# Attention of batches 1 to 3 with probabilities turned in blocks of 32 on VectorE and products over four row groups

## The chip, the cores and the metric

One core of a Trainium2 chip runs the whole kernel. Its engines are TensorE (matrix products into PSUM, 128 x 128), VectorE, ScalarE, GpSimd (POOL in the profile) and SyncE (SP), whose queue issues most transfers. They run on their own lists of instructions and meet only at semaphores. The metric is device time in microseconds (us), lower is better; the kernel before takes 131.04 us (median of 3 runs, 131.02 to 132.98).

## The reference

x has 4 batches of 512 tokens of 128 numbers, f32.

```python
# attention block
h = layernorm(x)                                  # over the last axis
q, k, v = h @ Wq + bq, h @ Wk + bk, h @ Wv + bv    # 128 -> 128
a = softmax(q @ k.T / sqrt(128)) @ v               # per batch, 512 x 512 scores
x = x + layernorm(a)
# mixture-of-experts block
h = layernorm(x)
spikes = sigmoid(h @ W_enc + b_enc)                # 128 -> 256
cont = spikes @ W_s2c + b_s2c                      # 256 -> 64
gate = two largest of softmax(cont @ Wr + br), scaled to sum 1, scattered over 8 experts
y = sum over e of gate[e] * (relu(cont @ W1[e] + b1[e]) @ W2[e] + b2[e])   # 64 -> 128 -> 64
d = sigmoid(y @ W_c2s + b_c2s) @ W_dec + b_dec     # 64 -> 256 -> 128
x = x + layernorm(layernorm(d) * ln_g + ln_b)
```

## The kernel before

**Tiling.** A batch is 4 groups (t) of 128 tokens. `x_in`, `x_mid` and the output keep tokens on the partitions; `xnT`, `yT`, `hT`, `spikes` and `cont` keep features on the partitions, turned by TensorE against an identity. All products are f32; an f32 product appears in the trace as two matmuls, each with its own weight load.

**Attention.** `project_y` makes yT, `project_v` v, `scores(b, t)` 128 x 512 scores in one of two PSUM banks. VectorE's `row_max` (L1200) takes the negative maximum, ScalarE's `exps` (L541) the exponentials with their sums, TensorE's `turn_probs` (L816) turns them as four squares of 128, ScalarE's `pT_out` (L546) copies them out of PSUM, and `attend` (L829) multiplies them with v: four products over 128 keys for each group. `attn_squares` (L552, ScalarE), `attn_var` (L1212, VectorE), a power of -1/2 on GpSimd (L431) and `mid_stats` (L1219, L1172 to L1177) add the normed result to x and take the statistics for the next norm.

**Experts.** `turn_h`, `encode` (L858), `to_cont`, `route` (L885), then `hidden_pair` (L918): the hidden layers of two experts, where two halves of the tokens lie on partitions 0 to 63 and 64 to 127. VectorE's `gate_hidden` (L1286) applies the bias, the relu and the gate, and `expert_out` (L942) sums eight experts in PSUM. `to_spikes`, `decode` (L971, L1002), `decode_scaled` and the two norms at the end follow. The router's gates go to HBM and come back spread over all partitions (`gate_all`, SP's queue). `router_top`, `router_index` and `router_gates` are VectorE's.

**Order.** Nothing is scheduled by a program: each engine's list of calls is written out by hand, and an engine never passes an instruction that waits. The batches are interleaved, so that attention of one batch stands between expert work of the batch two before it. An instruction waits for counts of semaphores (`wait_ge`), and so the order on one engine decides what the others get, and when. Small folds of biases (`b_cont`, `b_dec_sum`, `b2_plus`) are made on the way.

## Time and profile before

| | |
|---|---|
| median of 3 runs | 131.04 us |
| profiled execution | 130.91 us |
| its span | 129.0 us |
| TensorE busy | 118.7 us, 92% |
| VectorE busy | 94.4 us, 73% |
| ScalarE busy | 58.8 us, 46% |
| GpSimd busy | 33.8 us, 26% |
| granted TensorE clock, mean | 0.995 of full |

The span is the time from the first to the last recorded instruction of one profiled execution; the runs are timed around it. Busy time counts an engine's instructions, not its waits. Records of TensorE overlap, since one matmul begins while another ends: what a step costs is better read from the chain of waits, which goes back from the last instruction to what released it each time, or from the distance of two starts in the timeline. Groups by form give the mean length of one instruction. PE is TensorE, PEld its weight loads, DVE VectorE, ACT ScalarE.

### The profile page before, as it was taken

The page shows a single profiled execution, that of the slowest core. Times are in us where ns is not written, and L with a number is a line of the kernel's source. Part 1 is how long each engine was busy: PE and PEld are TensorE (multiplying, and loading weights), DVE is VectorE, ACT ScalarE, POOL GpSimd, SP SyncE. Part 2 cuts the span into 40 slices and gives each one's busy share as a digit, 9 for nine tenths or more (in the row PEclk, how much of TensorE's full clock was granted, in tenths as well). Part 3 has the DMA queues.
Part 4 walks back from the last instruction along what each step waited for, and adds up shares of the span by engine and source line. Part 5 has one row for each costly group of instructions (what it writes and reads, how often), then busy time and mean ns, then how long its engine had stood idle before and what let it go on. Part 6 is the DMA issues. An engine that isn't in the chain of part 4 may idle for free.

```text
span 129.0 us, 2501 instructions
## 1 busy us (share of the span) xinstructions
PE 118.7 (92%) x815; PEld 80.1 (62%) x815; DVE 94.4 (73%) x400; ACT 58.8 (46%) x173; POOL 33.8 (26%) x70
## 2 busy tenths in 40 slices
PE   6999999999999989999999999999998899998920
PEld 2556786878645767754575994657565455864910
DVE  0858537698989874788957168966889999389672
ACT  1647765556837575204666542053713003903620
POOL 4423503325231162220000132230081043330551
PEclk9999999999999999999999999999999999999998
DMA  3558800000000019700000198000019749720022
GB/s 113 132 121 227 234 18 3 0 0 3 0 5 0 0 50 324 290 8 0 0 0 0 41 293 329 3 0 0 8 48 319 299 138 323 276 86 0 4 79 81
DMA packets 9370, 12.42 MB, mean 96 GB/s; under 512 B 3169, under 2 KB 5998, under 8 KB 9358
## 3 DMA queue, kind: packets, MB, share of 16 engines
q1 hardware_dynamic: 8254, 12.08, 28.5%
q10 hardware_dynamic: 1104, 0.20, 0.8%
q8 instruction: 6, 0.10, 0.3%
q14 instruction: 6, 0.05, 0.1%
HBM read 11.16 MB, written 1.11 MB: 95 GB/s over the span
## 4 chain that ended last, share of the span: by engine, by line
PE 54%; DVE 23%; issue 8%; POOL 7%; ACT 3%; DMA 2%; POOLq 1%; DVEq 0%
PE ps_t L942 10%; POOL rstd L431 7%; PE ps_s L804 6%; PE ps_o L829 6%; PE ps_s L918 5%; PE ps_c L918 4%; DVE stats L1172 3%; PE ps_o L858 3%; PE ps_t L816 3%; DVE x_out L1366 2%; DMA x_in<-in_L_attn_x 2%; DVE xn L1184 2%; PE ps_o L918 2%; PE ps_a L769 2%; DVE neg_max L1200 2%
## 5 line engine op out<-in xcount | busy, mean ns | idle before, releaser
L431 POOL TENSOR_TENSOR rstd<-var_eps,minus_half 128x2 f32<-128x2 f32 (+1 forms) x33 | 25.4, 771 | 88.9 <-DVE var_eps L1177 47.3
L829 PEld LDWEIGHTS ps_o<-v,probsT 128*128 128x128 f32 x128 | 15.6, 191 | 4.6 <-ACT probsT L546 4.1
L829 PE MATMUL ps_o<-v,probsT 128*128 128x128 f32 x128 | 17.5, 279 | 0.4 <-ACT probsT L546 0.3
L942 PE MATMUL ps_t<-gated,w 128*64 128x256 f32 x128 | 17.0, 389 | 0.9 <-DVE gated L1286 0.8
L804 PE MATMUL ps_s<-xnT,yT 128*128 128x512 f32 x32 | 16.0, 596 | 0.1
L541 ACT ACTIVATE probs<-ps_s,neg_max 128x512 f32<-128x512 f32 x16 | 11.0, 687 | 11.1 <-DVE neg_max L1200 11.0
L1200 DVE TENSOR_REDUCE neg_max<-ps_s 128x1 f32<-128x512 f32 x16 | 10.9, 689 | 5.0 <-PE ps_s L804 4.9
L942 PEld LDWEIGHTS ps_t<-gated,w 128*64 128x64 f32 x128 | 8.0, 136 | 8.8 <-DVE gated L1286 4.2
L1286 DVE SCALAR_TENSOR_TENSOR gated<-ps_s,b_minus,gate_all 128x512 f32<-128x512 f32 x14 | 9.9, 744 | 1.9 <-PE ps_s L918 1.9
L546 ACT ACTIVATE probsT<-ps_t 128x512 f32<-128x512 f32 x16 | 9.5, 594 | 2.6 <-PE ps_t L816 2.4
L562 ACT ACTIVATE spikes<-ps_o,bias_half 128x512 f32<-128x512 f32 x6 | 4.1, 687 | 13.5 <-PE ps_o L858 13.4
L816 PE MATMUL ps_t<-ident,probs 128*128 128x128 f32 x64 | 9.8, 276 | 0.2 <-ACT probs L541 0.2
L816 PEld LDWEIGHTS ps_t<-ident,probs 128*128 128x128 f32 x64 | 7.3, 141 | 4.2 <-ACT probs L541 2.4
L1286 DVE SCALAR_TENSOR_TENSOR gated<-ps_c,b_minus,gate_all 128x512 f32<-128x512 f32 x12 | 8.4, 743 | 2.0 <-PE ps_c L918 2.0
L583 ACT ACTIVATE moeT<-ps_t 128x256 f32<-128x256 f32 x4 | 1.5, 384 | 14.5 <-PE ps_t L942 14.5
L918 PE MATMUL ps_s<-cont,w 64*128 64x256 f32 x56 | 7.9, 401 | 0.0
L804 PEld LDWEIGHTS ps_s<-xnT,yT 128*128 128x128 f32 x32 | 5.2, 191 | 2.7 <-issue 2.4
L1212 DVE SCALAR_TENSOR_TENSOR var_eps<-square_sum,eps_term 128x2 f32<-128x2 f32 x8 | 1.3, 165 | 7.1 <-ACT squares L552 6.9
L918 PE MATMUL ps_c<-cont,w 64*128 64x256 f32 x48 | 6.3, 380 | 0.0
L1219 DVE SCALAR_TENSOR_TENSOR x_mid<-ps_o,rstd,x_in 128x128 f32<-128x128 f32 x16 | 4.8, 343 | 2.0 <-POOL rstd L431 2.0
L918 PEld LDWEIGHTS ps_s<-cont,w 64*128 64x128 f32 x56 | 4.8, 186 | 2.1 <-issue 1.5
L1184 DVE TENSOR_SCALAR xn<-x_in,mean_var,rstd 128x128 f32<-128x128 f32 x16 | 5.2, 375 | 1.2 <-POOL rstd L431 0.9
(207 smaller groups left out, 218.6 us busy)
## 6 DMA issues: line engine op xcount, KB each, us to landing
gate_all<-gates SPq DMA_DIRECT2D x12, 512.0 KB, 6.0
gate_all<-gates SPq DMA_DIRECT2D x8, 256.0 KB, 3.6
x_in<-in_L_attn_x SPq DMA_DIRECT2D x3, 256.0 KB, 3.6
w<-in_L_ffn_W SPq DMA_DIRECT2D x3, 256.0 KB, 4.4
out<-x_out SPq DMA_DIRECT2D x3, 256.0 KB, 2.0
x_in<-in_L_attn_x SPq DMA_DIRECT2D x2, 128.0 KB, 2.5
out<-x_out SPq DMA_DIRECT2D x2, 128.0 KB, 1.7
w_enc<-in_L_ffn_W_enc SPq DMA_DIRECT2D x1, 128.0 KB, 2.7
```

The source lines that it names most:

```text
L431: nc.gpsimd.tensor_tensor(rstd[part], var_eps[part], minus_half[:, t0:t1], ALU.pow).then_inc(g_rstd[n], 1)
L541: nc.scalar.activation(probs[:, b % 2, t], ps_s[:, t % 2], ACT.Exp, bias=neg_max[:, b % 2, t:t + 1], accum_out=prob_sum[:, b % 2, t:t + 1] ...
L546: nc.scalar.activation(probsT[:, b % 2, t], ps_t[:, :].rearrange("p (k q) -> p k q", k=T), ACT.Identity).then_inc(a_pT, 1)
L804: nc.tensor.matmul(ps_s[:, t % 2], yT[:, b % 2, t * P:(t + 1) * P], xnT[:, b % 2], start=True, stop=True).then_inc(pe_s, 1)
L816: mm = nc.tensor.transpose(ps_t[:, k * P:(k + 1) * P], probs[:, b % 2, t, k * P:(k + 1) * P], ident[:, :])
L829: mm = nc.tensor.matmul(attn_out(t), probsT[:, b % 2, t, k], v[:, b % 2, k], start=(k == 0), stop=(k == T - 1))
L918: mm = nc.tensor.matmul(hidden_banks(b, e)[:, h], w1[half, e], cont[half, b % 2], start=True, stop=True)
L942: mm = nc.tensor.matmul(ps_t[h * M:(h + 1) * M, 0:SH], w2[:, e], gated[:, e, h * SH:(h + 1) * SH], start=False, stop=(e == E - 1))
L1184: nc.vector.tensor_scalar(result(t), source(t), mean_var[:, n, b % 2, t, 0:1], inv(n, b, t), ALU.subtract, ALU.mult).then_inc(done, 1)
L1200: nc.vector.tensor_reduce(neg_max[:, b % 2, t:t + 1], ps_s[:, t % 2], AX_X, ALU.max, negate=True).then_inc(v_max, 1)
L1219: nc.vector.scalar_tensor_tensor(x_mid[:, b, t], attn_out(t), inv(LN_ATT, b, t), x_in[:, b, t], ALU.mult, ALU.add).then_inc(v_mid, 1)
L1286: nc.vector.scalar_tensor_tensor(token_halves(gated[:, e]), hidden_banks(b, e), b1_minus[:, e:e + 1], token_halves(gate_all[:, b % 2, e]), ...
```

## The change

For batches 1 to 3 `turn_probs` and `pT_out` go. VectorE's `turn_blocks` transposes the 512 columns of one group's probabilities in squares of 32, which stay within their 32 partitions. With queries laid out in another order by `y_out`, this gives 16 pieces (`blocks[:, b % 2, j]`) in each of which every 32 partitions hold 32 keys against 128 queries. `attend(b)` is then 16 times four products of 32 rows, one for each quarter of the partitions; each quarter writes its own bank of `ps_o`, which has four banks now. Each quarter has to meet all keys, so v, with a column of ones that makes the sum of the probabilities, goes to HBM and comes back into all four quarters (`v_all`). ScalarE copies the result of a batch out of PSUM at once (`att_out`). Batch 0 stays as it was.

Along with it: for batches 2 and 3 the middle norm takes its squares on ScalarE (`mid_square`, `mid_var`, and `mid_add` in place of `mid_stats`); batch 0's last norm goes the way of batch 1's (ScalarE and GpSimd); bias folds stand together in `fold_biases`; output is written over `x_in`; PSUM banks are given out anew; and the lists of all engines are written in another order, in which scores and attention of a batch run ahead of the expert work of the one before.

```diff
+        v = sb("v", [P, 2, T, D + 1])
...
-        prob_sum = sb("prob_sum", [P, 2, T])
+        prob_sum = sb("prob_sum", [P, T])
...
-        probsT = sb("probsT", [P, 2, T, T, P])
+
+
+
+        blocks = sb("blocks", [P, 2, S // 32, T, 32])
+        v_all = sb("v_all", [P, 2, T, T, D + 1])
+
+        probsT = blocks[:, 0].rearrange("p (t a) b r -> p t a (b r)", t=T)
+        att = sb("att", [P, 2, T, D + 1])
```

```diff
+            sp.wait_ge(g_v_ones, 1)
+            for b in range(1, B):
+                sp.wait_ge(a_v, b + 1)
+                sp.dma_start(v_dram[b].ap(), v[:, b % 2].rearrange("p t d -> p (t d)")).then_inc(d_v_out[b], 16)
+                sp.wait_ge(d_v_out[b], 16)
+                if b == 3:
+                    sp.wait_ge(pe_o, 3)
+                for i in range(T):
+                    sp.dma_start(v_all[32 * i:32 * (i + 1), b % 2].rearrange("a j t d -> a j (t d)"),
+                                 v_dram[b].ap().rearrange("(j a) x -> a j x", j=T)).then_inc(d_v_all[b], 16)
 
             for b in range(B):
```

```diff
             def y_out(b):
                 for i, (bank, s0, s1) in enumerate(y_halves(b)):
                     act.wait_ge(pe_y, b + i + (b > 0) + 1)
-                    nc.scalar.activation(yT[:, b % 2, s0:s1], bank[:, s0:s1], ACT.Identity).then_inc(a_y, 1)
+                    if b == 0:
+                        nc.scalar.activation(yT[:, b % 2, s0:s1], bank[:, s0:s1], ACT.Identity).then_inc(a_y, 1)
+                    else:
+                        nc.scalar.activation(yT[:, b % 2].rearrange("d (t i r) -> d i t r", t=T, i=T),
+                                             bank[:, :].rearrange("d (i t r) -> d i t r", i=T, t=T),
+                                             ACT.Identity).then_inc(a_y, 1)
...
             def exps(b, t):
                 act.wait_ge(v_max, T * b + t + 1)
-                nc.scalar.activation(probs[:, b % 2, t], ps_s[:, t % 2], ACT.Exp, bias=neg_max[:, b % 2, t:t + 1],
-                                     accum_out=prob_sum[:, b % 2, t:t + 1]).then_inc(a_exp, 1)
-
-            def pT_out(b, t):
-                act.wait_ge(pe_pT, T * b + t + 1)
-                nc.scalar.activation(probsT[:, b % 2, t], ps_t[:, :].rearrange("p (k q) -> p k q", k=T),
+                nc.scalar.activation(probs[:, b % 2, t], ps_s[:, t % 2], ACT.Exp,
+                                     bias=neg_max[:, b % 2, t:t + 1],
+                                     accum_out=prob_sum[:, t:t + 1] if b == 0 else None).then_inc(a_exp, 1)
...
+            def att_out(b):
+                act.wait_ge(pe_o, b + 2)
+                if b == 3:
+                    act.wait_ge(v_mid, 2 * T)
+                nc.scalar.activation(att[:, b % 2], ps_o[:, :, 0:D + 1], ACT.Identity).then_inc(a_att, 1)
...
+            def mid_square(b, h):
+                act.wait_ge(v_mid, T * b + TH * (h + 1))
+                for t in range(TH * h, TH * (h + 1)):
+                    nc.scalar.activation(squares[:, b % 2, t], x_mid[:, b, t], ACT.Square, scale=-1.0,
+                                         bias=mean_var[:, LN_X, b % 2, t, 0:1],
+                                         accum_out=mid_square_sum[:, b % 2, t:t + 1]).then_inc(a_mid_square, 1)
```

```diff
+            def attend(b):
+                pe.wait_ge(v_blocks, T * b)
+                pe.wait_ge(d_v_all[b], 16 * T)
+                if b == 1:
+                    pe.wait_ge(v_mid, T)
+                    pe.wait_ge(a_square, T)
+                elif b == 2:
+                    pe.wait_ge(a_att, 1)
+                    pe.wait_ge(v_b2, 1)
+                    pe.wait_ge(v_bdec, 1)
+                    pe.wait_ge(v_bcont, 1)
+                    pe.wait_ge(v_logit, 1)
+                else:
+                    pe.wait_ge(v_gated, E)
+                for j in range(S // 32):
+                    for i in range(T):
+                        rows = slice(32 * i, 32 * (i + 1))
+                        mm = nc.tensor.matmul(ps_o[:, i, 0:D + 1], blocks[rows, b % 2, j].rearrange("p t r -> p (t r)"),
+                                              v_all[rows, b % 2, j % T, j // T],
+                                              start=(j == 0), stop=(j == S // 32 - 1))
+                mm.then_inc(pe_o, 1)
...
+            def fold_biases():
+                pe.wait_ge(a_att, 1)
+                pe.wait_ge(g_s2c, 1)
+                for h in range(2):
+                    for c in range(HC):
+                        mm = nc.tensor.matmul(ps_o[h * M:(h + 1) * M, 0, 0:1], w_s2c[:, c], ones[:, 0:1],
+                                              start=(c == 0), stop=(c == HC - 1))
+                pe.wait_ge(v_b1, 2)
+                pe.wait_ge(d_w2, 32)
+                for e in range(E):
+                    mm = nc.tensor.matmul(ps_o[0:E, 1, 0:M], b1_diag[:, e], w2[:, e], start=(e == 0), stop=(e == E - 1))
+                mm.then_inc(pe_b2, 1)
+                pe.wait_ge(v_wdec, 8)
```

```diff
+            def turn_blocks(b, t):
+                dve.wait_ge(a_exp, T * b + t + 1)
+                if b >= 2:
+                    dve.wait_ge(pe_o, b)
+                nc.vector.transpose(blocks[:, b % 2, :, t], probs[:, b % 2, t]).then_inc(v_blocks, 1)
```

ScalarE's list and part of TensorE's (its new calls):

```diff
+            att_out(1)
+            act.wait_ge(v_bias2, 2)
+            hT_out(0)
+            attn_squares(1, 0)
+            exps(2, 2)
+            attn_squares(1, 1)
+            spike(0, 0)
+            spike(0, 1)
+            exps(2, 3)
+            xnT_out(3)
+            cont_out(0)
+            y_out(3)
+            second_exp(0)
+            values_out(3)
+            att_out(2)
+            exps(3, 0)
+            attn_squares(2, 0)
```

```diff
+            project_y(2)
+            scores(2, 0)
+            project_v(2)
+            scores(2, 1)
+            attend(1)
             turn_h(0)
-            turn_probs(1, 3)
-            attend(1, 2)
+            fold_biases()
+            scores(2, 2)
             encode(0, 0)
             encode(0, 1)
-            attend(1, 3)
-            turn_x(2)
+            scores(2, 3)
             to_cont(0)
-            project_y(2)
+            turn_x(3)
             route(0)
-            scores(2, 0)
-            scores(2, 1)
-            project_v(2)
```

VectorE, from the middle of batch 1 to the first gated experts:

```diff
+            x_stats(3)
+            turn_blocks(2, 0)
+            turn_blocks(2, 1)
             attn_var(1, 0)
+            row_max(2, 2)
+            mid_stats(1, 0)
+            attn_var(1, 1)
+            x_norm(3)
+            row_max(2, 3)
+            mid_norm(1, 0)
+            mid_stats(1, 1)
...
+            turn_blocks(2, 2)
+            turn_blocks(2, 3)
+            mid_norm(1, 1)
+            router_top(0)
+            router_index(0)
+            router_gates(0)
+            row_max(3, 0)
+            attn_var(2, 0)
+            row_max(3, 1)
+            mid_add(2, 0)
+            attn_var(2, 1)
+            turn_blocks(3, 0)
+            mid_add(2, 1)
+            turn_blocks(3, 1)
+            mid_var(2, 0)
+            router_top(1)
+            row_max(3, 2)
+            gate_hidden(0, 0)
```

Places where the order moves, as the built programs have it. The first is TensorE around the projections of batch 3 (`xnT,w_a` is `project_y`, `wv,xnT` is `project_v`, `xnT,yT` a score, `ident,hn` a turn of h, `hT,w_enc` an encode, `w_r,cont` the route). Before:

```order
L777 MATMUL ps_a<-xnT,w_a 128x512
L829 MATMUL ps_o<-v,probsT 128x128 x4
L787 MATMUL ps_a<-wv,xnT 128x128 x4
L918 MATMUL ps_s<-cont,w 128x256 x4
L918 MATMUL ps_c<-cont,w 128x256 x4
L936 MATMUL ps_t<-gateT,b_plus 64x256 x2
L942 MATMUL ps_t<-gated,w 64x256 x8
L918 MATMUL ps_s<-cont,w 128x256 x4
```

and with the change:

```order
L948 MATMUL ps_o<-w_r,cont 128x8 x4
L827 MATMUL ps_a<-xnT,w_a 128x512
L837 MATMUL ps_a<-wv,xnT 128x128 x4
L894 MATMUL ps_o<-v_all,blocks 128x129 x64
L852 MATMUL ps_s<-xnT,yT 128x512 x2
L909 MATMUL ps_a<-ident,hn 128x128 x4
L923 MATMUL ps_o<-hT,w_enc 128x512 x2
L992 MATMUL ps_o<-cont,w 128x256 x4
L936 MATMUL ps_a<-spikes,w_s2c 64x256 x4
```

The projections stand behind the route of batch 0, batch 2's attention is one block of 64 products behind them, and the encode of batch 1 comes right after, ahead of all hidden experts; before, the turn of h of batch 1 had been made among the attention steps, and hidden experts came first.

The second is ScalarE at the same place (`hT` is the copy that an encode waits for, `squares` those of the attention norm, `att` the copy of the attention's result). Before, in the like place for batch 3's attention:

```order
L587 ACTIVATE spikes<-ps_c,bias_half 128x512 x2
L546 ACTIVATE probsT<-ps_t 128x512
L573 ACTIVATE e<-top_diff 128x4
L541 ACTIVATE probs,prob_sum<-ps_s,neg_max 128x512
L557 ACTIVATE hT<-ps_a 128x512
L546 ACTIVATE probsT<-ps_t 128x512
L578 DMA gates<-gate_blocks 4x32x32
```

and with the change, behind batch 2's attention:

```order
L634 ACTIVATE e<-top_diff 128x4
L578 ACTIVATE v<-ps_a 128x4x128
L597 ACTIVATE att<-ps_o 128x516
L584 ACTIVATE probs<-ps_s,neg_max 128x512
L605 ACTIVATE squares,square_sum<-att 128x128 x2
L639 DMA gates<-gate_blocks 4x32x32
L584 ACTIVATE probs<-ps_s,neg_max 128x512
L605 ACTIVATE squares,square_sum<-att 128x128 x2
L618 ACTIVATE hT<-ps_a 128x512
L623 ACTIVATE spikes<-ps_o,bias_half 128x512 x2
```

The copy of hT of batch 1 now has two exponentials and two pairs of squares ahead of it, all of which belong to batch 2 or 3.

The third is VectorE, where `b_cont` is made, for which ScalarE's first copy of `cont` waits. Before:

```order
L1200 TENSOR_REDUCE neg_max<-ps_s 128x1
L1219 SCALAR_TENSOR_TENSOR x_mid<-ps_o,rstd,x_in 128x128 x2
L1172 BN_STATS stats<-x_mid 128x6 x2
L1175 BN_AGGR mean_var<-stats 128x2 x2
L1177 TENSOR_SCALAR var_eps<-mean_var 128x2
L1200 TENSOR_REDUCE neg_max<-ps_s 128x1
L1408 TENSOR_SCALAR w_dec<-w_dec_raw,dec_mean 128x128 x2
L1411 TENSOR_TENSOR b_cont<-ps_c,bias_cols 128x1
L1414 TENSOR_SCALAR b_minus<-bias_cols 128x8
L1415 COPY b_diag<-bias_cols 128x8
```

and with the change:

```order
L1243 TENSOR_REDUCE neg_max<-ps_s 128x1
L1284 TENSOR_SCALAR hn<-x_mid,mean_var,rstd 128x128 x2
L1266 SCALAR_TENSOR_TENSOR x_mid<-att,rstd,x_in 128x128 x2
L1215 BN_STATS stats<-x_mid 128x6 x2
L1218 BN_AGGR mean_var<-stats 128x2 x2
L1220 TENSOR_SCALAR var_eps<-mean_var 128x2
L1505 TENSOR_TENSOR b_cont<-ps_o,bias_cols 128x1
L1507 SCALAR_TENSOR_TENSOR b_dec_sum<-b_dec_all,dec_mean,ps_o 128x128
L1511 TENSOR_TENSOR b_plus<-ps_o,b_rows 8x64
L1292 STREAM_TRANSPOSE blocks<-probs 128x16x32 x2
```

It stood behind the second maximum of batch 1 and stands now behind both middle blocks of batch 1.

## Rows read from the trace of the kernel before

**Rows 1.** The page, part 1: busy us, share of span, instructions.
```profile
PE 118.7 (92%) x815; PEld 80.1 (62%) x815; DVE 94.4 (73%) x400; ACT 58.8 (46%) x173; POOL 33.8 (26%) x70
```

**Rows 2.** The chain of waits, TensorE: start us, us, engine, tile, line, matmuls.
```profile
47.92 0.90 PE ps_o L829 x8
48.82 0.44 PE ps_t L816 x4
...
51.10 0.89 PE ps_a L787 x8
...
53.06 0.86 PE ps_c L918 x8
...
58.47 1.91 PE ps_o L858 x4
60.38 1.72 PE ps_s L804 x4
62.10 1.88 PE ps_t L942 x16
...
75.63 0.95 PE ps_o L829 x8
```

**Rows 3.** Timeline of weight loads (start us, us, ...); line 1033 (ns min/median/max).
```profile
17.71 0.32 PEld L1033 LDWEIGHTS ps_c<-ones,w_s2c 128*64 128x64 f32 x8
...
L1033 PEld LDWEIGHTS ps_c<-ones,w_s2c x8: 133/137/138, 17.7 to 17.9; 128*64 128x64 f32 x8
```

**Rows 4.** Timeline of VectorE, 31 to 40 us: start us, us, instruction, count.
```profile
31.43 1.11 DVE L1184 TENSOR_SCALAR xn<-x_in,mean_var,rstd 128x128 f32<-128x128 f32 x4 [0.45 <-POOL rstd L431]
...
36.71 0.61 DVE L1219 SCALAR_TENSOR_TENSOR x_mid<-ps_o,rstd,x_in 128x128 f32<-128x128 f32 x2 [0.33 <-POOL rstd L431]
37.35 0.49 DVE L1172 BATCH_NORM_STATS2 stats<-x_mid 128x6 f32<-128x128 f32 x2
...
38.09 0.17 DVE L1177 TENSOR_SCALAR var_eps<-mean_var 128x2 f32<-128x2 f32 x1
38.17 0.19 DVE L1232 TENSOR_TENSOR logits<-ps_c,br_all 128x32 f32<-128x32 f32 x1
...
38.88 1.28 DVE L1200 TENSOR_REDUCE neg_max<-ps_s 128x1 f32<-128x512 f32 x2
```

**Rows 5.** Groups by form: busy us, mean ns, idle before.
```profile
L546 ACT ACTIVATE probsT<-ps_t 128x512 f32<-128x512 f32 x16 | 9.5, 594 | 2.6 <-PE ps_t L816 2.4
...
L1299 DVE TENSOR_TENSOR z<-ps_a,g_all 128x512 f32<-128x512 f32 x2 | 1.4, 687 | 0.0
...
L1259 DVE TENSOR_TENSOR pick<-expert_no,top_no 128x32 f32<-128x32 f32 x8 | 1.2, 187 | 0.2
...
L1277 DVE STREAM_TRANSPOSE gate_blocks<-gate 128x32 f32<-128x32 f32 x4 | 0.8, 212 | 0.1
```

**Rows 6.** Timeline, 19 to 25 us: a score, its maximum, exponential, squares.
```profile
19.04 1.02 PE L804 MATMUL ps_s<-xnT,yT 128*128 128x512 f32 x2
...
20.10 0.69 DVE L1200 TENSOR_REDUCE neg_max<-ps_s 128x1 f32<-128x512 f32 x1 [0.83 <-PE ps_s L804]
...
23.02 0.69 ACT L541 ACTIVATE probs<-ps_s,neg_max 128x512 f32<-128x512 f32 x1 [0.92 <-DVE neg_max L1200]
...
24.17 0.28 ACT L552 ACTIVATE squares<-ps_o 128x128 f32<-128x128 f32 x1
...
24.58 0.22 ACT L552 ACTIVATION_READ_ACCUMULATOR squares<-ps_o 128x1 f32 x1
```

**Rows 7.** The chain of waits, VectorE: first and last step of batch 2's router.
```profile
89.06 0.20 DVE logits L1232
...
92.17 0.21 DVE gate_blocks L1277
```

**Rows 8.** Timeline: the last gated experts; page part 6: issues, KB, us to landing.
```profile
114.75 1.41 DVE L1286 SCALAR_TENSOR_TENSOR gated<-ps_o,b_minus,gate_all 128x512 f32<-128x512 f32 x2 [0.59 <-PE ps_o L918]
...
gate_all<-gates SPq DMA_DIRECT2D x8, 256.0 KB, 3.6
```

More of the change, by code:

```diff
@@ L259, in attention_moe_block @@
         d_ln = sem("d_ln")
+        d_v_out = [sem(f"d_v_out{b}") for b in range(B)]
+        d_v_all = [sem(f"d_v_all{b}") for b in range(B)]
         d_gateT = [sem(f"d_gateT{i}") for i in range(2)]
@@ L464, in _ @@
                 inverse_std(LN_MID, 1, h)
-            inverse_std(LN_X, 3, 0)
+            for h in range(2):
+                inverse_std(LN_ATT, 2, h)
+            for h in range(2):
+                inverse_std(LN_MID, 2, h)
             pool.wait_ge(v_wdec, 8)
@@ new lines, in _ @@
+            exps(3, 1)
+            attn_squares(2, 1)
+            hT_out(1)
+            spike(1, 0)
+            spike(1, 1)
+            mid_square(2, 0)
+            cont_out(1)
+            exps(3, 2)
+            mid_square(2, 1)
+            second_exp(1)
+            exps(3, 3)
+            hT_out(2)
+            spike(2, 0)
+            spike(2, 1)
+            gate_out(1)
+            moe_out(0)
+            att_out(3)
+            attn_squares(3, 0)
+            cont_out(2)
+            spike2(0, 0)
@@ L1039, in _ @@
-            attend(0, 2)
+            turn_probs(3)
+            attend_first(2)
             scores(1, 1)
-            turn_probs(1, 0)
-            attend(0, 3)
+            attend_first(3)
             scores(1, 2)
-            turn_probs(1, 1)
-            attend(1, 0)
-            pe.wait_ge(v_wdec, 8)
-            pe.wait_ge(v_bias, 1)
-            for c in range(HC):
-                mm = nc.tensor.matmul(ps_c[:, 0, 0:D], ones[:, :], w_dec[:, c], start=(c == 0), stop=(c == HC - 1))
-            mm.then_inc(pe_bdec, 1)
@@ new lines, in _ @@
+            project_y(3)
+            project_v(3)
+            attend(2)
+            scores(3, 0)
+            scores(3, 1)
+            turn_h(1)
+            encode(1, 0)
+            encode(1, 1)
+            hidden_pair(0, 0)
+            to_cont(1)
+            scores(3, 2)
+            route(1)
+            expert_biases(0)
+            hidden_pair(0, 1)
+            scores(3, 3)
+            for e in range(4):
+                expert_out(0, e)
+            turn_h(2)
+            hidden_pair(0, 2)
@@ new lines, in _ @@
+            hidden_pair(0, 3)
+            encode(2, 0)
+            encode(2, 1)
+            for e in range(4, E):
+                expert_out(0, e)
+            attend(3)
+            to_cont(2)
+            to_spikes(0)
+            route(2)
+            hidden_pair(1, 0)
+            expert_biases(1)
+            hidden_pair(1, 1)
+            decode(0)
+            for e in range(4):
+                expert_out(1, e)
+            hidden_pair(1, 2)
+            turn_h(3)
+            hidden_pair(1, 3)
@@ L1122, in _ @@
             expert_out(1, 4)
             expert_out(1, 5)
-            to_cont(2)
+            encode(3, 0)
+            encode(3, 1)
             expert_out(1, 6)
             expert_out(1, 7)
-            route(2)
+            to_cont(3)
+            to_spikes(1)
             hidden_pair(2, 0)
-            to_spikes(1)
-            encode(3, 0)
-            encode(3, 1)
-            decode(1, 0)
-            decode(1, 1)
-            to_cont(3)
-            decode(1, 2)
-            decode(1, 3)
@@ L1148, in _ @@
-            expert_out(2, 7)
+            to_spikes(2)
             hidden_pair(3, 1)
-            to_spikes(2)
             expert_biases(3)
-            decode_part(2, 0)
+            for e in range(4):
+                expert_out(3, e)
+            decode(2)
             hidden_pair(3, 2)
-            expert_out(3, 0)
-            expert_out(3, 1)
             hidden_pair(3, 3)
-            for e in range(2, E):
+            for e in range(4, E):
                 expert_out(3, e)
@@ L1160, in _ @@
             for h in range(2):
-                decode_part(3, h)
+                decode(3, h)
             for h in range(2):
@@ L1482, in _ @@
-            attn_var(3, 1)
-            for e in range(1, 4):
-                gate_hidden(1, e)
-            mid_stats(3, 1)
-            mid_norm(3, 0)
+            attn_var(3, 0)
+            mid_add(3, 0)
+            attn_var(3, 1)
+            router_top(2)
+            mid_add(3, 1)
+            gate_hidden(1, 0)
+            gate_hidden(1, 1)
+            router_index(2)
+            mid_var(3, 0)
+            gate_hidden(1, 2)
+            mid_var(3, 1)
+            router_gates(2)
+            mid_norm(3, 0)
@@ L1513, in _ @@
             z_means(1, 0)
+            scaled_weights()
             for e in range(E):
```

592 lines of the change are left out of this document (243 added, 349 removed).

## The prediction

> **What bounds the kernel now.** I read four views, in this order. The page's busy line [rows 1]: TensorE works 92% of the span, VectorE 73%, ScalarE 46%. The chain of waits [rows 2] is mostly TensorE in its middle, and gives what TensorE's steps cost when they follow each other: attention of one group of tokens 0.90 us, its turn 0.44, one pair of hidden experts 0.86, two scores 1.72, two encodes of the same columns behind a change of mode 1.91, four expert outputs 1.88. The timeline [rows 3, 4, 6, 7] gives the pace inside a step, which is a little less than the mean length of one instruction, because ends overlap. The groups by form [rows 5] give lengths that no step isolates. The reader is to see that TensorE is the bound, and that it can be only because VectorE and ScalarE are always one step ahead of it. The profiled execution took 130.91 us with a span of 129.0, so 1.9 lie around the span; the median of the runs is 131.04.
>
> **The change, part by part.**
>
> *Turns off TensorE.* Twelve turns of probabilities go (batches 1 to 3): 12 x 0.44 = 5.3 us of TensorE [rows 2]. ScalarE loses their 12 copies, 12 x 0.59 = 7.1 us [rows 5]. It gains three copies of the attention's result (0.6 each by the same row), squares for the middle norms of batches 2 and 3 (0.63 for two with their sums: 24.17 to 24.80 [rows 6]) and batch 0's last normalisation. At 46% its total decides nothing; its order does, below.
>
> *The new attention.* 64 products of 32 rows for each batch. An f32 product runs as two matmuls, here of 129 columns; before, eight matmuls of 128 took 0.90, so 0.112 each. Two row groups do run side by side: eight matmuls of 256 columns took 0.86, where four of 512, the same columns in sequence, took 1.72 [rows 2]. Four abreast, a batch is 128 x 0.112 / 4 = 3.6 us; two abreast 7.2; one at a time 14.3. I take 3.6. Four abreast need a new matmul every 0.028 us, and eight tiny ones were issued in 0.32 less the last one's own 0.14, so 0.026 apart [rows 3]. That is the nearest row, and it is close. So attention costs TensorE what it cost (4 x 0.90).
>
> The Trainium skill ("TensorE: Matmul & The Clock Gate", Part 3, the table of measured speedups) has four row tiles at 3.07 times, not 4. By that a batch takes 4.7 us and the sum grows by about 3. No row here has four groups.
>
> *Turns on VectorE.* Twelve block transposes of 512 columns. Those of the trace have 32: 212 ns, where arithmetic on 32 columns takes 187 and on 512 takes 687 [rows 5]. That is 1.04 ns a column, so 212 + 480 x 1.04 = 0.71 us. If instead all above a base of 147 were columns, 2.0 ns each, it would take 1.2; below, nothing of 512 columns paces under 0.6 [rows 4]. I take 0.71, in sequence 0.66, because the longer base fits what 32 columns show beside their neighbour. VectorE gets 12 x 0.66 = 7.9 us, loses the statistics of eight groups (0.74 a pair by the rows from 37.35 to 38.09, so 3.0) and batch 0's last centring and sum, some 2.5: net +2.4 on 94.4. Again the place decides, since six of the turns fall before 40 us.
>
> *v through HBM.* Out 264 KB once, back four times 264 KB; a 256 KB fetch took 3.6 us to land [rows 8], and as the four share the engines I put both ways at 8 to 10 us together. In the walk below each v is ready 13 us or more before its use: nothing. Without that cover it would be up to 8 us. The gate fetches stand behind these on SP's queue; the last v fetch is through by about 58, when batch 0's gates leave: nothing.
>
> *Memory shared anew* (x_in as output, one ps_o of four banks): nothing, their readers are long done; if one were not, a wait of one step, 0.9.
>
> **The walk.** The engines hand work to each other in another rhythm now, so I follow the new order with these prices. Up to 17.5 us nothing differs.
>
> (a) *To the end of batch 2's attention.* VectorE from 17.5: statistics of x 1.3, five maxima 3.2, four turns 2.6, x norm 1.1, two middle blocks of 1.46 (36.71 to 38.17), small ones 1.1, and 2.8 of waits for scores: the fourth turn of batch 1 ends at 32.5 [rows 4]. Its attention: 32.5 to 36.3, copied by 37.2, then the bias folds 1.6 and a score, and the next maximum starts at 40.0. From there VectorE has 0.65 + 1.46 + 0.3 + 1.1 + 0.6 + 0.55 + 1.46 = 6.1 ahead of b_cont, which is now formed last: 46.1. cont of batch 0 waits for b_cont on ScalarE, route for cont, and batch 3's projections stand behind route on TensorE: 0.5 + 0.5 + 0.9 + 0.8 for the copy + 0.9, so 49.7. Batch 2's attention: 49.8 to 53.4. Before, that attention and batch 3's v were both through at 52.0 [rows 2]. With 8 turns, 3.5 us, saved, it is 1.4 later, and the turn of h of batch 1 (0.44), done before, is still to come.
>
> (b) *Behind it.* encode(1) needs hT(1), which ScalarE copies only after this: score 0.9 and 0.2 to land, maximum 0.65, exponential 0.65, squares 0.63, a small VectorE step 0.2, the second maximum 0.65, exponential 0.65, squares 0.63, the copy 0.6, together 5.8 [rows 2, 4 to 6]. TensorE has 2.2 of work in between, stands for 3.6, and goes on at 59.2.
>
> (c) *To the end of batch 3's attention.* encode 1.7, hidden 0.9, cont 0.9, a score 0.9 and route with its copy: 64.1. VectorE: top of the router 0.7 and 0.2 to land, 65.0; then to the last gated expert of batch 0 eight gated 5.4 (0.68 each [rows 8]), two turns and two maxima 2.6, middle norms 1.1, index 0.6, the router's gates 1.5 (a whole router took 89.06 to 92.38, some of it a wait [rows 7]; I take 2.8), 0.15: 76.4. Its product ends at 77.6 behind an encode, attention at 81.4. Before, this was 76.6 [rows 2]. What is left for TensorE then is 1.1 more now (to_spikes and decode of batch 0 against an encode).
>
> (d) *To the last gated expert.* TensorE has 12 hidden pairs 10.3, 24 expert outputs 11.3, three decodes 6.0, an encode 1.7, five steps of 0.86, routes, biases and a turn 2.5: 36.1, with some 2.2 for changes of mode (0.19 between 1.91 and 1.72, less for short steps) 38.3, to 119.7. To this come hand-offs where VectorE is late: gated(1,3) behind the gates of router 2, 2.5; gated(2,4) to (2,7) behind router 3 and a scaling, 1.6; scaled_weights, now ahead of all of batch 3's, 2.5: 6.6 in all, so the last gated expert ends at 125.8. Before it ended at 116.2 [rows 8], 39.6 after the attention. At that stretch's losses it would now be 81.4 + 39.6 + 1.1 = 122.1.
>
> (e) *The end.* Before, 116.2 to 129.0 = 12.8; less the scaling of batch 2, which now stands ahead: 12.2.
>
> Sum: 125.8 + 12.2 = 138.0 of span, or 134.3 by the milder form of (d); with 2.0 around it up to the median, 140.0 and 136.3. I forecast **138**, between them: 5% slower.
>
> **The rivals.** *TensorE alone is still the bound* and the waits of (a) to (d) are covered; this one ends on the other side. The 5.3 us of turns fall out, six changes of mode (0.19) are added: 131.0 - 5.3 + 1.1 = 126.8. The 92% speak for it. It decides from the point where the wait before encode(1) is under 0.5 us, and a chain of ten steps stands there: 14%.
>
> *The late part wins the early loss back*: batch 2's attention ends at 53.4, but (b) overlaps and (d) runs without late hand-offs. Then attention of batch 3 ends at 77 to 79, and 38.3 + 12.2 + 2 behind it give 130 to 132: 13%.
>
> *Row groups go only two abreast*, or the sequencer can't feed four: 3.6 more for each batch, 10.7, part of it in TensorE's idle time of (a): 145 to 149. The pace of 0.026 speaks against it: 8%.
>
> *Dear transposes*: 12 x 0.5 = 6, two thirds of it on the chain: 142. The trace has none beyond 32 columns: 9%.
>
> My forecast keeps 56%. That the change isn't done can be left out: the order of instructions has the twelve transposes and three times 64 products in their places.
>
> **How the numbers follow.** A difference of 2% is about what can be told from none here. Slower by over 2%: 0.56 + 0.08 + 0.09 = 0.73; within 2%: 0.13; faster: 0.14. The range goes from 130, where the win-back ends, to 143, which takes in dear transposes; outside lie TensorE as the only bound and most of two abreast, some 20% together.
>
> **What would show it.** Right: 3.6 to 4.0 us for a batch's attention in the chain; transposes of 0.7; TensorE idle for 3 us or more before encode(1), waiting for hT, and some 2 before batch 0's route; the last gated expert past 121. Wrong: batch 2's attention over before 51, encode(1) within a microsecond of the turn of h, or waits for gated experts no longer than before.

## The result, and the profile after

The changed kernel takes 152.97 us (median of 5 runs, 151.99 to 157.02) against 131.04 (5 runs, 130.95 to 132.98): a ratio of 1.165 [1.160, 1.171]. It is 16.5% slower; 138 was forecast, 5% slower, and the range ended at 143. The direction was right, the time was not. Some executions of a kernel run longer at a lower granted clock (157.02 us here, at 0.896 where the other four had 0.922 to 0.927); the ratios leave them out.

The changed kernel was profiled again beside the experiments, in an execution of 152.87 us (span 151.1), and all its rows here are from that one. The page, part 1 and the row of the granted clock (tenths, 40 slices of 3.8 us):

```profile
PE 124.3 (82%) x1054; PEld 78.5 (52%) x1054; DVE 96.2 (64%) x387; ACT 57.8 (38%) x172; POOL 34.8 (23%) x72
...
PEclk9999999599999689959977999996999999999985
```

TensorE's share fell from 92% [rows 1] to 82%, yet it is busy 5.6 us longer, though 5.3 us of turns are gone, and its idle time grew from 10.3 us (129.0 - 118.7) to 26.8. The clock row says why it is busy for longer: it dips five times before the end. The chain of waits, in order of time (start us, us, engine, tile, line, count):

```profile
33.76 3.83 PE ps_o L894 x128
...
47.16 0.16 DVE b_cont L1505
47.41 0.48 ACT cont L630
47.93 0.61 PE ps_o L948 x8
...
50.29 2.07 PE ps_a L837 x8
52.36 4.43 PE ps_o L894 x128
56.80 1.07 PE ps_s L852 x2
...
62.05 0.50 ACT hT L618
62.59 2.49 PE ps_o L923 x4
...
83.92 1.88 PE ps_t L1013 x16
85.80 3.78 PE ps_o L894 x128
```

L894 is the new attention: 3.8 us a batch, as forecast. Batch 3's v (L837, x8) takes 2.07 us, the same work as 0.89 in [rows 2]: it ran at the lower clock. So did part of the attention behind it and of the encode at 62.59. The windows table shows the clock beside TensorE's busy time (us, then busy and count of PE, PEld, DVE, ACT, POOL, then clock):

```profile
26.00:30.00 4.00, 4.00 (x8) 1.54 (x8) 2.35 (x8) 1.39 (x3) 0.06 (x1) 0.57 0.59 117
30.00:44.00 14.00, 13.01 (x183) 8.85 (x184) 10.42 (x42) 6.52 (x18) 2.96 (x4) 1.00 0.39 96
...
77.00:81.00 4.00, 3.74 (x18) 2.49 (x20) 2.07 (x11) 0.60 (x1) 0.00 (x0) 0.57 0.00 0
81.00:86.00 5.00, 5.00 (x38) 2.57 (x38) 4.03 (x10) 1.53 (x3) 0.00 (x0) 1.00 0.02 3
```

A mean of 0.57 over 4 us is 3.4 us at 1.2 GHz and 0.6 at 2.4. With 48 to 58, 61 to 72 and 100 to 110 us (0.83; 0.87 and 0.83; 0.83) the lower level holds for 17 us. What comes ahead of each stretch is in the list of waits, the last of which end at 25.9, 47.9, 62.6, 77.3 and 100.0 us (engine and tile, whom it waited for: us, times, longest):

```profile
PE ps_t L1013 <- DVE gated L1352: 7.5, 6, 1.9
PE ps_o L923 <- ACT hT L618: 3.4, 1, 3.4
PE ps_o L948 <- ACT cont L630: 2.3, 1, 2.3
PE ps_a L819 <- DVE xn L1227: 2.2, 1, 2.2
```

The end, on the chain:

```profile
129.96 1.80 PE ps_a L1051 x16
...
131.96 0.97 ACT squares L661 x7
132.93 1.53 ACT z L668 x4
134.53 1.26 POOL x_in L470
135.79 0.25 POOL b_z_hi L518
...
138.31 1.03 POOL rstd L459
```

z of batch 1 (L668) could have been normalised from 125.5 us on, when POOL had its factors ready and ScalarE was about to stand idle until 131.8, but it stands in ScalarE's list behind the squares of batch 2's decode; POOL adds it, then forms the bf16 parts of b_z (2.4 us), and only then batch 2's rstd.

### The profile page after: what moved, and what is told of

Same layout as the page of the kernel before. It is cut to its first block, busy times and chain, and to the rows that moved or that the text cites. A ratio compares the mean times of both kernels' runs of the same rounds, so it can differ in the third digit from the quotient of the medians.

```text
span 155.2 us, 2982 instructions
## 1 busy us (share of the span) xinstructions
PE 128.5 (83%) x1054; PEld 81.1 (52%) x1054; DVE 96.2 (62%) x387; ACT 57.9 (37%) x172; POOL 34.8 (22%) x72
## 4 chain that ended last, share of the span: by engine, by line
PE 58%; DVE 21%; ACT 7%; POOL 5%; issue 4%; DMA 2%; POOLq 1%; ACTq 0%; DVEq 0%
PE ps_o L894 9%; PE ps_s L852 7%; PE ps_o L992 6%; PE ps_t L1013 6%; DVE gated L1352 4%; DVE neg_max L1243 3%; PE ps_a L827 3%; POOL rstd L459 3%; PE ps_a L837 2%; PE ps_s L923 2%; PE ps_o L923 2%; PE ps_a L1051 2%; DVE stats L1215 2%; PE ps_a L936 2%; DMA w_qkv<-in_L_attn_Wk 2%
## 5 line engine op out<-in xcount | busy, mean ns | idle before, releaser
L1352 DVE SCALAR_TENSOR_TENSOR gated<-ps_o,b_minus,gate_all 128x512 f32<-128x512 f32 x24 | 16.8, 743 | 7.8 <-PE ps_o L992 7.8
L992 PE MATMUL ps_o<-cont,w 64*128 64x256 f32 x96 | 15.8, 464 | 0.0
L894 PEld LDWEIGHTS ps_o<-v_all,blocks 32*128 32x128 f32 x384 | 13.0, 215 | 1.4 <-DVE blocks L1292 0.8
L894 PE MATMUL ps_o<-v_all,blocks 32*128 32x129 f32 x384 | 13.6, 302 | 0.0
L992 PEld LDWEIGHTS ps_o<-cont,w 64*128 64x128 f32 x96 | 10.4, 225 | 4.7 <-issue 2.6
L923 PE MATMUL ps_o<-hT,w_enc 128*128 128x512 f32 x8 | 5.7, 846 | 3.4 <-ACT hT L618 3.4
L1292 DVE STREAM_TRANSPOSE blocks<-probs 128x512 f32<-128x512 f32 x12 | 8.2, 696 | 0.0
L1051 PEld LDWEIGHTS ps_a<-w_dec,spikes 128*128 128x128 f32 x48 | 5.9, 192 | 0.1
L1051 PE MATMUL ps_a<-w_dec,spikes 128*128 128x128 f32 x48 | 5.8, 275 | 0.0
L1352 DVE SCALAR_TENSOR_TENSOR gated<-ps_s,b_minus,gate_all 128x512 f32<-128x512 f32 x8 | 5.7, 741 | 0.0
```

The costliest lines, as they stand in the source:

```text
L894: mm = nc.tensor.matmul(ps_o[:, i, 0:D + 1], blocks[rows, b % 2, j].rearrange("p t r -> p (t r)"), v_all[rows, b % 2, j % T, j // T], star ...
L923: nc.tensor.matmul(enc_bank(b, c), w_enc[:, c * P:(c + 1) * P], hT[:, b % 2], start=True, stop=True).then_inc(pe_enc, 1)
L992: mm = nc.tensor.matmul(hidden_banks(b, e)[:, h], w1[half, e], cont[half, b % 2], start=True, stop=True)
L1051: mm = nc.tensor.matmul(decoded(b, t), spikes2[:, b % 2, c, t * P:(t + 1) * P], w_dec[:, c], start=False, stop=(c == HC - 1 and t == t1 - 1))
L1292: nc.vector.transpose(blocks[:, b % 2, :, t], probs[:, b % 2, t]).then_inc(v_blocks, 1)
L1352: nc.vector.scalar_tensor_tensor(token_halves(gated[:, e]), hidden_banks(b, e), b1_minus[:, e:e + 1], token_halves(gate_all[:, b % 2, e]), ...
```

## The experiments

Times are medians; beside these kernels the kernel before took 131.2 to 131.3 us, and gains are counted from the 152.87 of the changed kernel's second profile. Theories: **clock** (TensorE's gaps are followed by stretches at 1.2 GHz, for which my sum had no term), **order** (hand-offs late by the place of an instruction in a list), **end** (POOL's and ScalarE's last lists), and the rival, that **the new operations** themselves (products, transposes) cost.

**Gaps filled.** 58 products of zeros, as the warm-up's, at seven places (12 + 10 of them among the expert outputs of batches 0 and 1; the 48 of the text below leaves ten out). One of the places:

```diff
+ def fill(bank, count):
+     for _ in range(count):
+         nc.tensor.matmul(bank, zeros[:, 0:P], zeros[:, :], start=True, stop=True)
  pe.wait_ge(a_att, 2)
+ fill(ps_o[:, 0], 12)
  encode(1, 0)
```

> The changed kernel with 48 bf16 products of zeros (128x512, as the warm-up's) in TensorE's gaps: 8 before turn_x(2), 4 before scores(2,0), 8 before route(0), 4 before project_v(3), 12 before encode(1,0), 12 between the first four expert_out of batch 0 and 10 before expert_out(1,2) and (1,3). Each writes a bank that stands free and that the next product there overwrites; nothing is left out. Changed kernel: 152.5 us. Clock theory (TensorE is granted 1.2 GHz after each of five gaps, and some 27 us of the trace pass at that level, in which TensorE is behind by about half): the PEclk row shows 9 all through from the start to the last 5 us and the time falls by 8 to 13 us, to 140 to 144. Order theory (the lists make TensorE late, the clock only shows it): the gaps are as long as before, the clock may be up, but what follows a gap waits on the other engines anyway: 150 to 153. If the fillers only cost (48 by 0.2 us, those that don't fit in their gap): 153 to 158.

147.20 us, 1.122 [1.114, 1.130]: 5.7 less than the changed kernel, from work that computes nothing. The row of the clock, and the attention of batches 2 and 3 in its chain:

```profile
PEclk9999999999999999999999999999999999995599
...
49.96 3.78 PE ps_o L900 x128
...
79.58 3.78 PE ps_o L900 x128
```

Attention of batch 3 ends at 83.4 instead of 89.6. Nothing but the fillers and the clock differs up to there, and the fillers compute nothing, so the clock is shown to cost about 6 us. The first 1.5 of them are less certain (attention 1 starts at 32.29 for 33.76): other executions, below, kept the clock behind that first gap without a filler. The gain misses the 8 to 13 expected, which counted 27 us at the lower level from the 157.02 us execution; the one of 152.87 has 17, worth 8.5 at most. By the last gated expert the gain is 7.2 us (130.0 for 137.1), and 0.6 is lost behind it, where this kernel has a dip of its own.

**Two hand-offs earlier.**

```diff
  row_max(2, 2)                  # VectorE
+ dve.wait_ge(pe_bdec, 1)
+ (b_cont)
  mid_stats(1, 0)
  attend(2)                      # TensorE
+ turn_h(1)
  scores(3, 0)
  att_out(2)                     # ScalarE
+ hT_out(1)
  exps(3, 0)
```

> The changed kernel with two moves: b_cont with its wait for pe_bdec on VectorE right after row_max(2,2) (it stood 5 us later, behind mid_stats(1,1)), and turn_h(1) on TensorE ahead of scores(3,0) with ACT's hT_out(1) right behind att_out(2). Order theory: the gap of 2.4 us before route(0) shrinks to 1 or less and that of 3.6 us before encode(1,0) goes: 5 to 6 us less by the gaps alone, 146.5 to 148. Clock theory adds that the two falls that follow them (47.7 to 58 us and 64.8 to 71.6 us) go too, worth another 5 to 8 us: 139 to 143. If it is the attention or the transposes themselves that cost, the time stays at 150 to 153.

145.21 us, 1.108 [1.100, 1.116]: 7.7 less. The wait for hT(1) is gone from the list, that for cont is 1.4 instead of 2.3, and the clock's row has lost the dips at 48 and 61 us:

```profile
PEclk9999999999999999999789999959999999997797
...
49.24 3.78 PE ps_o L894 x128
```

More than the gaps (0.9 + 3.4) came back, as the clock theory said, but the time lies between the ranges of the two theories (139 to 143 and 146.5 to 148): a shallower one follows at 68 to 75 us, and one at 93. And 1.3 us are not the moves' own: the gap before turn_x(2), the same in both kernels, is followed by a dip at 26 us in the changed kernel and by none here, so attention 1 starts at 32.44 for 33.76. That leaves 6.4 for the moves.

**The end's order.**

```diff
  spike2(2, c)                   # ScalarE
+ z_norm(1)
  dec_square(2, 0)
- z_norm(1)
- scaled_weights()               # VectorE, ahead of gate_hidden(3, *)
+ scaled_weights()               # ahead of attn_var(3, 0)
  (b_z chain on POOL: ahead of inverse_std(LN_DEC, 0, 0))
```

> The changed kernel with the end's order alone changed: VectorE's scaled_weights ahead of attn_var(3,0) (it stood ahead of batch 3's gated products), POOL's b_z chain ahead of the LN_DEC of batch 0, and ACT's z_norm(1) ahead of dec_square(2,0). Tail theory (z_norm(1) behind dec_square(2,0) holds POOL's z_add(1), and behind it stand 2.5 us of b_z chain and the rstd of batch 2): 2.1 us from the gated products of batch 3 and about 4 us behind decode(2): 145.5 to 148. Theory that the end is set by TensorE's late products alone: at most the 2.1 us of VectorE, 150 to 151.5. If the moved work only delays batch 3's attention norms: 152 to 155.

Four runs took 147.49, 148.52, 152.50 and 153.73 us. The first, which was profiled, and the second are 4 to 5 less than the changed kernel; two are too few for an interval, and the rows have to answer. POOL's timeline:

```profile
126.90 1.27 POOL L470 TENSOR_TENSOR x_in<-z,x_mid 128x512 f32<-128x512 f32 x1 [1.76 <-ACT z L668]
132.57 1.02 POOL L459 TENSOR_TENSOR rstd<-var_eps,minus_half 128x4 f32<-128x4 f32 x1 [4.39 <-DVE var_eps L1372]
```

The sum of batch 1 comes 7.6 us earlier and batch 2's rstd waits for its variance, not for POOL. From the last gated expert to the end it is 11.9 us (133.8 to 145.7), where the changed kernel has 14.0 (137.1 to 151.1). The last gated experts:

```profile
132.40 1.40 DVE L1352 SCALAR_TENSOR_TENSOR gated<-ps_s,b_minus,gate_all 128x512 f32<-128x512 f32 x2
```

against, in the changed kernel:

```profile
135.73 1.40 DVE L1352 SCALAR_TENSOR_TENSOR gated<-ps_s,b_minus,gate_all 128x512 f32<-128x512 f32 x2
```

Of the 5.4 us between the spans 2.1 is the end, and 2.6 lies between the end of attention 3 and the last gated expert (88.8 to 133.8 for 89.6 to 137.1), where `scaled_weights` was moved away. The rest, 0.7, was there before any move, in an execution that kept its clock at 26 us. So the moves themselves are worth 4.7.

**Both sets of moves.**

> The moves of the two kernels before this one together. If gaps, clock and tail are separate causes, the gains add: 152.5 less 9 to 14 (order with clock) less 5 to 7 (tail) is 132 to 138, the forecast's own 138 at the upper end. If the order moves are worth their gaps alone, 140 to 143. If neither matters, 150 or more.

140.64 us, 1.074 [1.066, 1.081]: 12.2 less, nearly the sum of the two (7.7 and about 5): by the rows 6.4 and 4.7 from the moves, and 1.3 from the dip at 26 us, which this execution did not have either. The gains add, but each was smaller than expected: not 132 to 138, but the low end of the range for moves worth their gaps alone. A dip at 70 us remains, and one at 90 to 97.

**Both, and its gaps filled** (34 products of zeros).

> Both moves of the kernel before (140.6 us) with 34 products of zeros in the gaps that it still has: 8 before turn_x(2), 5 before route(0), 12 between the first expert_out of batch 0, 9 before expert_out(1,3). That kernel's trace shows 1.2 GHz at about 67 to 72 us and 94 to 99 us, some 6 us in all. Clock theory: 9 all through in the PEclk row and 2 to 3 us less, 137.5 to 139. Order theory (the waits of the lists decide what is left): 140 to 141. Fillers that don't fit: over 141.

137.83 us, 1.047 [1.036, 1.058], and 9 in all slices of the clock but the last (the page is of an execution of 139.31 us). 2.8 us less, as the clock theory said.

**Fewer transposes.** Both moves, without turn_blocks of batches 2 and 3:

```diff
- turn_blocks(2, *), turn_blocks(3, *)
- pe.wait_ge(v_blocks, T * b)
+ pe.wait_ge(v_blocks, T)
+ pe.wait_ge(a_exp, T * (b + 1))
```

> Both moves (140.6 us) without VectorE's eight block transposes of batches 2 and 3: their attention reads the blocks of batches 0 and 1, so the probabilities of those two batches are left out of the result. It takes 8 by 0.70 us = 5.6 us off VectorE. Theory that the transposes on VectorE are what delays the hand-offs (norms, gated products, router) around 42 to 75 us: 3 to 5 us less, 136 to 138. Theory that VectorE has room beside TensorE and the order of the lists decides: 139.5 to 141.

1.086 [1.071, 1.101]; the two runs that the ratio rests on took 140.39 and 141.34 us, against 140.64: with 5.6 us less work on VectorE nothing is won. One thing hides in this: the profiled execution has the dip at 27 us, which that with both moves has not, and attention 2 starts 1.5 us later for it (50.75 for 49.29). So the transposes may be worth up to some 1.5 us, but not the 3 to 5 of their theory; each took 0.70 us:

```profile
L1292 DVE STREAM_TRANSPOSE blocks<-probs 128x512 f32<-128x512 f32 x12 | 8.2, 697 | 0.0
```

(that row is of the changed kernel: busy us, mean ns, idle before.)

**One hole in the kernel before.**

```diff
  act.wait_ge(v_max, T * b + t + 1)          # exps(2, 2)
+ act.dma_start(hole[:, :], bq...).then_inc(d_hole, 16)
  (attend(2, 0), TensorE)
+ pe.wait_ge(d_hole, 16)
```

> The kernel before the change (131.0 us) with one hole: TensorE waits ahead of attend(2,0), where its trace has no gap over 0.5 us for 20 us, for a small DMA that ACT issues once row_max(2,2) is done; nothing is left out. The gap should be 2.5 to 4 us. Clock theory: the granted clock, which never falls in that kernel until its last microseconds, falls to 1.2 GHz behind the hole for some 3 us, and the time rises by the gap and 1.5 to 2 us more, 135 to 137, unless waits further down take part of it back. Theory that the fall has another cause than a gap (what kind of products run, four row groups): the clock stays up, and the time rises by the gap or less, 132 to 135.

**The same hole, filled** with 12 products of zeros.

> The kernel before with the same hole and 12 bf16 products of zeros (some 2.6 us at full clock) in it. Clock theory: the clock stays up, and the time is 1.5 to 2 us below that of the empty hole. If the clock doesn't matter, both are alike, within 0.5 us.

135.36 us, 1.031 [1.021, 1.042], and 134.09, 1.023 [1.010, 1.036]. The step behind the hole, then 46 to 50 us, first empty:

```profile
45.61 1.38 PE L835 MATMUL ps_o<-v,probsT 128*128 128x128 f32 x8 [3.69 <-DMA hole<-in_L_attn_bq]
...
46.00:50.00 4.00, 4.00 (x18) 3.18 (x17) 0.00 (x0) 1.19 (x2) 0.91 (x2) 0.57 0.01 2
```

and filled:

```profile
45.81 1.16 PE L837 MATMUL ps_o<-v,probsT 128*128 128x128 f32 x8 [0.70 <-DMA hole<-in_L_attn_bq]
...
46.00:50.00 4.00, 4.00 (x32) 3.46 (x31) 1.26 (x4) 1.62 (x3) 1.20 (x3) 1.00 0.03 6
```

In a kernel with none of the change's operations a gap of 3.7 us alone brings the clock down: TensorE is busy all 4 us in both, and does 18 matmuls in one, 32 in the other. The medians differ by 1.3 us and the spans by 1.4, a little below the 1.5 to 2 expected. The two intervals overlap, but the mean clock was 0.977 to 0.981 in the four runs with the empty hole and 0.989 to 0.999 in the four with the filled one. The hole costs 4.1 us empty and 2.8 filled.

**The products one after another.** Both moves, with attend's loops exchanged, so that neighbours share their 32 rows:

```diff
- for j in range(S // 32):
-     for i in range(T):
+ for i in range(T):
+     for j in range(S // 32):
```

> The kernel with both moves (140.6 us) with the two loops of attend exchanged: all 16 products of a row group, then those of the next, so that no two that follow one another stand on different rows. The same products, loads and bytes, nothing left out. In the kernel with both moves one batch takes 3.85 us. If the overlap of products on different rows is what makes 64 products of 32 rows no dearer than 16 of 128, one batch now takes 12 to 15 us, and the time is about 3 by 9 to 11 us longer, 160 to 172, less what falls into gaps. If it made no difference, 3.9 us a batch and 140 to 141.

205.06 us (one run): further than expected, since here the clock falls with no gap ahead. The chain's step for batch 1, and its windows:

```profile
32.36 20.45 PE ps_o L894 x128
...
36.00:38.00 2.00, 2.00 (x23) 2.00 (x20) 0.11 (x1) 0.00 (x0) 0.00 (x0) 1.00 1.04 239
38.00:42.00 4.00, 4.00 (x25) 4.00 (x24) 0.00 (x0) 0.00 (x0) 0.00 (x0) 0.51 0.74 149
42.00:46.00 4.00, 4.00 (x23) 4.00 (x24) 0.00 (x0) 0.00 (x0) 0.00 (x0) 0.50 0.00 0
```

The overlap is real: 3.8 us side by side, 20.5 in sequence. At the upper clock the sequence would take 128 x 0.112 = 14.3 us [rows 2], and the first 5.6 us have its pace, so four abreast is about 3.8 times as fast.

**Batch 0's router ahead of attention 1**, as before the change.

> The kernel with both moves (140.6 us) with batch 0's encoder and router ahead of attention 1, as they were before the change: turn_h(0), scores(2,2), encode(0,*), fold_biases, to_cont(0), scores(2,3), turn_x(3), route(0), attend(1) on TensorE, VectorE's and ACT's lists in the same order, gate_out(0) ahead of att_out(1). In the kernel with both moves route(0) runs at 45.8 us, the first gate_all lands after 64 us, and TensorE waits for gated products 0.7, 2.6 and 0.5 us between 66 and 70 us. Late-gates theory: route(0) at about 41, the gate_all there before hidden_pair(0,0), these gaps and the fall of the clock behind them gone: 4 to 6 us less, 135 to 137. Theory that batch 0's place doesn't matter, as TensorE has other work meanwhile: 139.5 to 141. If attention 1, now 5 to 8 us later, holds batch 1's encoder: 142 to 145.

142.28 us, 1.083 [1.073, 1.093]: not faster than 140.64, so the late-gates theory fell as it stood; the value is in the range of the third, and TensorE now waits 1.7 us for hn before batch 1's turn of h. route(0) ran 5 us earlier and its gates left 10 us earlier, but SyncE's queue and VectorE's list did not use them (the chain's row of gate_out, the timelines of SyncE and VectorE):

```profile
45.25 1.07 ACTq L639
...
52.82 1.73 SPq L418 DMA_DIRECT2D v_all<-v  x4
54.65 0.28 SPq L429 DMA_DIRECT2D gateT<-gates  x1
54.97 2.23 SPq L431 DMA_DIRECT2D gate_all<-gates  x5
...
65.38 0.74 DVE L1357 SCALAR_TENSOR_TENSOR gated<-ps_o,b_minus,gate_all 128x512 f32<-128x512 f32 x1
```

The fetch stands behind v_all(3). That does not wait for attention 2, as the next text has it: in the kernel it needs `pe_o` at 3, the end of attention 1, and in the trace SyncE's queue stood 13.2 us for v(3), which ScalarE had ready at 50.0, and 2.4 for its way to HBM. The first gated expert stands behind router_top(1).

**Batch 0's experts first**: the fetch ahead of v_all(3), its hidden pairs, gated products and outputs ahead of encode(1,*) and router_top(1).

```diff
+ fetch_gates(0)                 # SyncE, ahead of sp.wait_ge(pe_o, 3)
  scores(3, 0)                   # TensorE
+ hidden_pair(0, 0); hidden_pair(0, 1); expert_biases(0)
  turn_h(1)
  ...
+ (expert_out(0, *), hidden_pair(0, 2), hidden_pair(0, 3))
  encode(1, 0)
```

> The kernel of the early router (142.3 us) with batch 0's experts ahead of batch 1's encoder and router, as before the change: SyncE fetches batch 0's gates ahead of v_all(3) (whose issue waits for attention 2), TensorE runs hidden_pair(0,*) and expert_out(0,*) from behind scores(3,0) on and encode(1,*) behind them, VectorE the eight gated(0,*) from behind row_max(3,0) on, router_top(1) behind them. In the early-router kernel route(0) ran 5 us earlier and its gates left at 45 us, but the first gated product stood behind router_top(1) on VectorE and the fetch behind v_all(3) on SyncE, and it came at 65.4 us all the same. Theory that the place of batch 0's experts is what the rest of the loss is: the last gated product of batch 0 comes at 62 to 66 us instead of 76 to 78, TensorE's gaps at 66 to 71 us go, and the time is 133 to 137. Theory that the work only changes places (batch 1's encoder now comes late in its stead, with gaps of its own at 60 to 75 us): 140 to 145.

138.00 us, 1.054 [1.045, 1.062], the fastest without fillers: 2.6 less than both moves alone and 4.3 less than the early router. Batch 0's last gated expert comes at 68.0 (76.4 with both moves, 60.9 before the change), and the clock stays up, in this execution: three took 137.96 to 138.04 us at a mean clock of 0.992 to 0.994, the fourth 139.36 at 0.980. The page's row, attention 3, and the last gated experts of all:

```profile
PEclk9999999999999999999999999999999999999997
...
76.74 3.79 PE ps_o L899 x128
...
122.51 1.40 DVE L1364 SCALAR_TENSOR_TENSOR gated<-ps_s,b_minus,gate_all 128x512 f32<-128x512 f32 x2
```

That is later than its theory's 62 to 66 and 133 to 137, and better than its rival's 140. The fetch itself went only 1.8 us earlier (52.86 for 54.65), since it still stands behind v(3)'s way to HBM. Against the kernel before, attention 3 ends 4.0 us later (80.5 for 76.6), from there to the last gated expert it is 3.8 more (43.4 for 39.6), and the end is 0.5 shorter.

**The changed kernel again**, whose rows stand above.

> The changed kernel itself once more, beside the others on one chip, for its profile. All theories: 151 to 154 us, with the granted clock at 1.2 GHz behind each gap of over 2 us on TensorE (about 26, 48, 65, 80 and 104 us), a clock of about 0.92 over the span.

152.87 us, clock 0.926, the gaps where they were expected.

No version beats the kernel before.

## Why the prediction was wrong, by its own steps

**Turns, attention, transposes** were right. Attention 3.8 us a batch for 3.6; the trace bears out four groups abreast. Its 3.8 times is not the 3.07 of the Trainium skill's table ("TensorE: Matmul & The Clock Gate", Part 3), which is for 512 columns where this kernel has 129; the 4.7 us estimated from it no batch took at the upper clock. Transposes 0.70 for 0.71. Fewer of them won at most 1.5 us. v through HBM never held TensorE.

**(a) and (b), the hand-offs**, were right in kind. b_cont at 47.2 for 46.1; TensorE stood 3.4 us before encode(1) for 3.6, and from the score at 56.80 to the encode at 62.59 it was 5.8, the 5.8 forecast. What failed is what stood around them: attention 2 ended at 56.8, not 53.4.

**The step that failed is one that the sum does not have: TensorE's clock in the stretches behind its waits.** I priced each step of (a) to (d) by rows of a kernel whose clock never fell in its middle, while the same walk took gaps of 2 and 3.6 us into TensorE's work. With the gaps filled, attention 2 is at 49.96 to 53.74, where 49.8 to 53.4 was forecast, and attention 3 ends at 83.4 for 81.4. The fall costs 5.7 us of the 14.9 by which the forecast missed (152.87 less 138). Which of the gaps brings it was partly chance: the first, before turn_x(2), not in every execution.

**(c)** came at 89.6 for 81.4; 6.2 of the 8.2 is that clock, 2.0 is left. With the gaps filled, encode(2) ends at 77.7, and four expert outputs stand whole behind it in TensorE's list (1.9 us), where the walk had the last of them end at 77.6.

**(d)** was 44.4 us long by the sum; 47.5 in the changed kernel (89.6 to 137.1), 46.6 with the gaps filled. (Its own terms, 38.3 and 6.6, add up to 44.9: the walk says 125.8 where 126.3 comes out.) scaled_weights was priced rightly: with it moved, the stretch is 45.1 with both moves, where it was 47.6 with the hand-offs alone. The stretch was under-sized by 2.2, by which of the other hand-offs no run separates, and its milder form, by which I had taken 2 us off the sum of 140.0, had nothing for it.

**(e)** was 12.2 and measured 14.0, with the gaps filled 14.6 (a dip at 130 to 137 us lies in it, so some 0.6 of this is clock too); with the lists mended 11.9. I carried the old end over, less one scaling, and did not follow POOL, which now forms b_z and batch 2's rstd behind z_add(1).

Together, from 138: clock 5.7, (a) to (c) 2.0, (d) 2.2, (e) 2.4, the 2.0 taken off: 14.3 of 14.9. The 0.6 left is not in the walk: the kernel with the gaps filled has a median of 147.20 over a profiled execution of 146.50, and I take its clock term from the median and the others from the profile.

**The rivals.** TensorE alone as the bound had the right size for what it saves, but its point of decision, a wait under 0.5 us before encode(1), was never near: 3.4 us here. Nor does it hold where its point is met: with the hand-offs moved, the wait for hT is gone, and with the end mended too the kernel takes 140.64 us, not 126.8. Nor did the late part win anything back: it lost more. No rival went above 149.

**Why it is slower at all.** The saving is 5.3 us of TensorE's work that it had only while it was fed. Mending the two hand-offs and the end takes back 12.2 of the 21.7 us (1.3 of it the dip at 26 us), and batch 0's experts in their old place 2.6 more. That leaves 7, half of it before attention 3 ends and half between there and the last gated expert. Why, is argued and not shown: four banks of PSUM for one attention force batch 0's encoder and bias folds to one side of it, and each batch's probabilities must all be turned before its first product, where 16 small attentions used to fill gaps.

## What to carry to other kernels

Do not price a gap on TensorE by its length alone where the steps behind it were measured at the upper clock: here a gap of 3.7 us cost 4.1, and 2.8 with products of zeros in it; in the changed kernel such products gave back 5.7. After any move, read the lists of the engines that look idle, POOL and SyncE too: at 23% busy, POOL and the order on ScalarE held the end for 2 us, and with the gates early, their fetch went 9.4 us behind them, where 4.2 were enough with the queue free, because it stood behind a transfer that waited for something else. Here 5.3 us of work taken off the bound were worth nothing, since the other engines did not keep it fed.

## What the runs showed of the hardware

- The dips are alike: 0.57 over 4 us behind different gaps of two kernels. Gaps filled with products of zeros kept 2.4 GHz. Which gap is followed by a dip stays open, and the program alone does not decide it. Behind the gap of 2.2 us before turn_x(2) the clock fell in both profiles of the changed kernel and in the one with fewer transposes, and not in the other six that have this gap unfilled. In the three that fell, two products of `w_qkv` at 5 us (L794), before any of these gaps, took 0.63 to 0.64 us, in the six 0.39 to 0.49: there the clock had come up later at the start. That the two hang together is seen, not tested.
- The clock also fell with TensorE busy for 4.00 of 4.00 us, in products of 32 rows one after another (0.51 and 0.50); the same products four abreast kept it.
- Four products on 32 rows each run fully side by side, with loads of their own: 128 f32 matmuls of 129 columns in 3.8 us.
